# A graph network on one core: one group of edges in five picked by one-hot products, picked rows summed by two additions, lines compared two groups ahead

## What is computed

```
# layer 0, per edge: msg from the source row, weighted by a score of both rows and the relation
a   = tanh(relu(sum((x[src] @ A1.T + b1) * (x[dst] @ A2.T + b2 + rel_emb[etype])) / sqrt(32)))
nei = segment_sum(a * (w_comp[etype] x basis weights applied to x[src]), dst)
x   = layernorm(x + relu(nei + x[src[last edge of the node]] @ self_loop))
x   = layernorm(x + segment_sum(x[src], dst))                    # layer 1
x   = layernorm(x + softmax attention over the edges of a node)  # layer 2
x   = layernorm(x + 10 steps of normalised propagation)          # layer 3
```

## Time and profile before

| | |
|---|---|
| median of 3 runs | 1260.72 us (1260.57 to 1262.55) |
| profiled execution, its own time | 1265.35 us |
| its span, first to last instruction | 1263.6 us |
| mean granted TensorE clock | 0.778 |
| busy: TensorE, VectorE, ScalarE, GpSimd | 977.7, 1020.9, 638.0, 698.4 us |
| first scores of the sweep (L1285) | 63.03 us |
| last gather issued | 912.1 us |
| load of the sums issued (L527) | 929.18 us |

### The profile page before, as it was taken

One profiled execution on the slowest core, in us unless ns is written; L12 is line 12 of the kernel. 1 busy time (PEld: TensorE's weight loads), 2 busy tenths in 40 slices (PEclk: granted clock), 3 DMA queues, 4 the chain that ended last, 5 costly groups with the idle time before them and its releaser, 6 DMA issues.

```text
span 1263.6 us, 58393 instructions
## 1 busy us (share of the span) xinstructions
PE 977.7 (77%) x23808; PEld 898.6 (71%) x23808; DVE 1020.9 (81%) x3443; ACT 638.0 (50%) x1731; POOL 698.4 (55%) x686
## 2 busy tenths in 40 slices
PE   2368788788788787787788677767827995999996
PEld 2357677677677676676677566666726995999996
DVE  8679999889888988898889888888844997655556
ACT  1146666656565555565566555555688980000000
POOL 5777777777777777777777777777600000000000
PEclk9557777777777767767777777767758997999998
DMA  4522222122222221122122212221100000000001
GB/s 108 73 46 56 51 46 46 46 48 48 47 46 46 46 45 45 45 46 45 45 46 46 44 46 45 45 45 41 18 14 3 3 4 3 4 4 4 4 4 18
DMA packets 55896, 46.32 MB, mean 37 GB/s; under 512 B 37442, under 2 KB 51837, under 8 KB 55624
## 3 DMA queue, kind: packets, MB, share of 16 engines
q1 hardware_dynamic: 34056, 31.45, 8.9%
q0 software_dynamic: 21568, 11.09, 6.9%
HBM read 40.19 MB, written 2.28 MB: 34 GB/s over the span
## 4 chain that ended last, share of the span: by engine, by line
PE 25%; DMA 21%; DVE 17%; issue 14%; SPq 11%; POOL 10%; ACT 1%; DVEq 0%; POOLq 0%; ACTq 0%
PE ps L820 12%; POOL arena L587 10%; DMA arena<-line_table 10%; DMA agg_table<-arena 8%; PE ps L762 3%; SPq L519 3%; SPq L496 3%; PE ps L728 3%; DMA arena<-x_pad,arena 3%; DVE arena L1271 2%; SPq L520 2%; SPq L500 2%; DVE arena L1465 2%; DVE arena L1269 1%; PE ps L709 1%
## 5 line engine op out<-in xcount | busy, mean ns | idle before, releaser
L587 POOL DMA_INDIRECT arena<-x_pad,arena x674 | 696.5, 1033 | 205.8 <-issue 200.3
L728 PE MATMUL ps<-arena 128*32 128x44 f32 (+3 forms) x7832 | 204.9, 234 | 152.5 <-DVE arena L1300 152.1
L728 PEld LDWEIGHTS ps<-arena 128*32 128x32 f32 x7832 | 152.4, 133 | 192.7 <-DVE arena L1300 167.3
L1271 DVE TENSOR_SCALAR arena<-pair_no,arena 128x275 bf16<-128x275 f16 (+2 forms) x784 | 239.2, 308 | 0.0
L820 PE MATMUL ps<-arena,adj_words 128*128 128x64 f16 (+1 forms) x6250 | 195.7, 193 | 24.5 <-DVEq L1415 21.8
L820 PEld LDWEIGHTS ps<-arena,adj_words 128*128 128x128 fp8e4 x6250 | 193.5, 98 | 26.6 <-DVEq L1415 22.6
L1300 DVE TENSOR_TENSOR arena<-ps,arena 128x768 f32<-128x768 f32 x196 | 188.0, 959 | 6.7
L709 PE MATMUL ps<-arena 128*128 128x175 bf16 (+3 forms) x1567 | 164.0, 261 | 31.3 <-DVE arena L1271 30.4
L762 PE MATMUL ps<-aggT 128*128 128x128 bf16 x2268 | 175.3, 244 | 0.0
L1015 ACT ACTIVATE arena<-arena 128x4 f32<-128x4 f32 x196 | 40.2, 205 | 266.7 <-DVE arena L1286 255.9
L762 PEld LDWEIGHTS ps<-aggT 128*128 128x128 bf16 x2268 | 159.2, 112 | 0.0
(11 more groups left out here) (213 smaller groups left out, 1261.7 us busy)
## 6 DMA issues: line engine op xcount, KB each, us to landing
arena<-line_table SPq DMA_DIRECT2D x28, 602.0 KB
arena<-x_pad,arena POOLq DMA_INDIRECT x674, 3.3
arena<-line_table SPq DMA_DIRECT2D x28, 140.0 KB
arena<-pick_table SPq DMA_DIRECT2D x27, 128.0 KB
arena<-dst_parts SPq DMA_DIRECT2D x196, 5.7 KB
agg_table<-arena SPq DMA_DIRECT2D x196, 2.5 KB
dst_parts<-aggT SPq DMA_DIRECT2D x1, 735.0 KB, 14.7
x<-x_pad SPq DMA_DIRECT2D x1, 400.0 KB
```

The lines of the kernel that those rows point to most:

```text
L587: pool.indirect_dma_start(to, None, table, bass.IndirectOffsetOnAxis(ap=index, axis=0)).then_inc(done, 16)
L728: return nc.tensor.matmul(to.rearrange("p (d m) -> p d m", m=MIX_COLS)[:, :, 0:m1 - m0], rows_of_slot, factors[:, :, m0:m1], start=False, ...
L1271: last = v.tensor_scalar(pair_hot[:, h, k, 0:n], pair_no[:, 0:n], pair_of[:, g, k:k + 1], None, ALU.is_equal)
```

## The change

One group in five is picked instead of one in seven: groups 7, 12, ..., 192, 38 in place of 27. The order within a pick is as before, but the reading of picked rows now stands ahead of the next one-hots, and both bursts of one-hots move by one group, to the first two groups of each five. The code loads of SyncE leave the branch of the line loads and come every fifth group. The reduction L1324 becomes two additions. Lines are compared two groups ahead instead of four.

```diff
-LINE_AHEAD = 4
+LINE_AHEAD = 2
-PICK_AT, PICKS = LINE + 3, LINES - 1
-PICKED = range(PICK_AT, PICK_AT + PICKS * LINE, LINE)
+PICK_EVERY, PICK_LEAD = 5, 2
+PICK_AT = PICK_EVERY + PICK_LEAD
+PICKED = range(PICK_AT, GROUPS, PICK_EVERY)
+PICKS = len(PICKED)
-HOTS_AT = ((1, range(0, 4)), (2, range(4, PICK_DEEP)))
+HOTS_AT = ((0, range(0, 4)), (1, range(4, PICK_DEEP)))
...
                         if c >= 1:
                             load_lines(c)
-                        if c < PICKS:
-                            if c >= 2:
-                                sp.wait_ge(pick_hots, c - 1)
-                            sp.dma_start(codes[:, c % 2, :], pick_table[c:c + 1, :].to_broadcast([P, WINDOW]))\
-                              .then_inc(code_in[c % 2], 16)
+                    if g % PICK_EVERY == 0 and g // PICK_EVERY < PICKS:
+                        c = g // PICK_EVERY
+                        if c >= 2:
+                            sp.wait_ge(pick_hots, c - 1)
+                        sp.dma_start(codes[:, c % 2, :], pick_table[c:c + 1, :].to_broadcast([P, WINDOW]))\
+                          .then_inc(code_in[c % 2], 16)
...
-                    if g // LINE < PICKS and g % LINE >= LINE - SLOTS:
-                        pick_tile(g // LINE, g % LINE - (LINE - SLOTS))
+                    if g // PICK_EVERY < PICKS and g % PICK_EVERY >= PICK_EVERY - SLOTS:
+                        pick_tile(g // PICK_EVERY, g % PICK_EVERY - (PICK_EVERY - SLOTS))
...
-                    link(v.tensor_reduce(xp[:, PICKED[c] % AHEAD, :, 0:FEAT],
-                                         picked.rearrange("p (k w f) -> p k f w", k=SLOTS, w=PICK_WIDE), AX.X, ALU.add))
+                    of = picked.rearrange("p (k w f) -> p k w f", k=SLOTS, w=PICK_WIDE)
+                    half = PICK_WIDE // 2
+                    link(v.tensor_tensor(of[:, :, 0:half], of[:, :, 0:half], of[:, :, half:PICK_WIDE], ALU.add))
+                    link(v.tensor_tensor(xp[:, PICKED[c] % AHEAD, :, 0:FEAT], of[:, :, 0, :], of[:, :, 1, :], ALU.add))
...
+                    if g % PICK_EVERY == 0 and 1 <= g // PICK_EVERY <= PICKS:
+                        read_picked(g // PICK_EVERY - 1)
                     for group, (at, _) in enumerate(HOTS_AT):
-                        if g % LINE == at and g // LINE < PICKS:
-                            make_pick_hots(g // LINE, group)
-                    if g % LINE == 0 and 1 <= g // LINE <= PICKS:
-                        read_picked(g // LINE - 1)
+                        if g % PICK_EVERY == at and g // PICK_EVERY < PICKS:
+                            make_pick_hots(g // PICK_EVERY, group)
                     make_mixed(g)
```

More of the change, by code:

```diff
@@ L1211, in _ @@
             dve.sem_inc(codes_made, 1)
-            link(v.tensor_scalar(pick_of, block_of[:, PICK_AT::LINE, :][:, 0:PICKS, :], PICK_WIDE - 1, None, ALU.bitwise_and))
+            link(v.tensor_scalar(pick_of, block_of[:, PICK_AT::PICK_EVERY, :], PICK_WIDE - 1, None, ALU.bitwise_and))
             for w in range(PICK_WIDE):
@@ L1822 @@
         "x_pad": x_pad, "edges": edges,
-        "src_cols": columns(grouped[:, 0]), "pick_rows": grouped[:, 0].reshape(GROUPS, WINDOW)[PICK_AT::LINE][:PICKS], "dst_cols": columns(grouped[:, 1]), "next_cols": columns(after), "bases": bases,
+        "src_cols": columns(grouped[:, 0]), "pick_rows": grouped[:, 0].reshape(GROUPS, WINDOW)[PICK_AT::PICK_EVERY], "dst_cols": columns(grouped[:, 1]), "next_cols": columns(after), "bases": bases,
         "dst_rows_in": grouped[:, 1].reshape(LINE_ROWS, -1), "rel_rows_in": grouped[:, 2].reshape(LINE_ROWS, -1),
```

## The result

The changed kernel takes 1252.20 us (median of 6 runs, 1248.47 to 1255.37) beside 1260.99 for the kernel before (6 runs, 1258.91 to 1263.63): a ratio of 0.9926, 95% interval 0.9905 to 0.9948, or 8.8 us less. Its profiled execution took 1252.85 us, with a span of 1250.6 and a mean granted clock of 0.842 (1263.6 and 0.778 before).

What follows compares the result with a forecast made beforehand. SyncE's queue, whose line loads hold its stores, was taken to set the end. Start -4.3, last line-load wait -1.7, tail -4, code loads -1 gave -11: 1260.7 - 11 = 1249.7 us, range 1236 to 1261.5.

Steps and rivals of the forecast that it cites:

- The start: SyncE's early line loads, up to the one at 180.52 us: issued 4.3 us earlier, bounds 1 and 6.
- The lines' lead: Lines compared two groups ahead: VectorE's 7.0 us wait in group 3 goes, so SyncE's early line loads come earlier.
- The added picks: One more set of one-hots and extra reading of picked rows by group 20: 2.7 us off the start's gain.
- The cycles: SyncE's 22 line-load cycles: -1.7 us for the wait before the last line load, -1 for the moved code loads.
- The tail: SyncE's 25 stores after the last line load: 4 us less waiting, bounds 0 and 7.6.
- The gathers' end: GpSimd's gathers end near 874 us: 44 fewer save 55, 11 more one-hot sets cost 16, so 39 gained.
- VectorE's wait for the sums: At the sweep's end VectorE waits for the sums longer than 10.97 us, by 15 us or more.
- The rule on two additions: Two-input additions contend with GpSimd's reads: 0.70 us in each of 38 picks, 27 us more for the gathers.
- The new wait: SyncE's code loads wait for VectorE's one-hots: expected to end before it starts; seeing such waits would show the forecast wrong.
- B: Rival: the gathers' relief is passed on, the end moves with the sweep by -19 to -39 us, 1222 to 1242; chance 0.12.
- C: Rival: nothing is left, code loads cost 0.8 us in the open, tail gains nothing; 1258 to 1263 us; chance 0.16.
- D: Rival: slower, TensorE at 1.2 GHz sets the pace, 4.44 us a group; 1273 us or more; chance 0.08.

Runs made afterwards that it cites:

- e1_lines4: The changed kernel with lines compared four groups ahead again instead of two; 1258.44 us, ratio to before 0.9980.
- e9_picks_alone: The changed kernel with lines four groups ahead and the single reduction, leaving only one group in five picked; 1260.37 us, ratio to before 0.9994.
- e10_one_in_six: The changed kernel with one group in six picked instead of one in five; 1252.88 us, ratio to before 0.9934.
- e2_old_lines2: The kernel before with lines compared two groups ahead as its one edit; 1260.12 us, ratio to before 0.9989.
- e4_old_split: The kernel before with each line load of 86 partitions issued as 80 and 6; 1257.59 us, ratio to before 0.9972.
- e3_split: The changed kernel with each line load of 86 partitions issued as 80 and 6; 1224.84 us, ratio to before 0.9711.

## Why the prediction came out

**The bound was right.** In all twelve kernels the span ends 334 to 336 us after SyncE's load of the sums (929.18 to 1263.6 before, 915.52 to 1250.6 after, 864.33 to 1199.8 in the fastest). In the changed kernel that load follows SyncE's queue: making the queue longer costs its full time, taking its hold away gains 27.4 us, and VectorE's 11.7 us and 24 gathers cost nothing.

**The start** (predicted -4.3 us): measured -4.15 at the sixth line load. Its two parts can be read apart. The lines' lead gives 182.39 - 176.37 = 6.0 to 184.24 - 179.14 = 5.1 (7.0 predicted). The added picks take 182.39 - 180.52 = 1.9 with the additions (2.7 predicted), and 184.24 - 180.52 = 3.7 with the reduction, for which the prediction's prices give 2.0 + 1.71 = 3.7. So with the additions the two parts were priced 1.0 and 0.8 us too high and the errors cancel; the match to 0.2 us is in part luck.

**The cycles** (-1.7 for the wait before the last line load, -1 for the code loads): measured -2.84 over the 22, with no wait at a line load over 0.2 us. One execution of each does not settle so small a difference: `e1_lines4`, with the same code loads, took 668.38 us for these cycles where the changed kernel took 673.67.

**The tail** (-4, with 0 and 7.6 as bounds): measured -6.7 from the last line load on, of which 41.33 - 35.51 = 5.8 in the 25 stores. It lies nearer the upper bound; in `e9_picks_alone`, where only the picks differ from before, it is 923.35 - 856.62 = 66.7 us, so 5.4 of the 6.7 come with the picks.

**The median** was predicted at 1249.7 and is 1252.2, for a reason that the sum does not hold. I took the sum from the profiled execution, 4.6 us above the median of its kernel, and carried that offset over. The profile after came out at 1252.85, below the 1254.3 predicted for it, but only 0.65 above its median. So part of what the change took from the profile of before was not there in the ordinary run. The predicted 11 us lie between the 12.5 of the two profiles and the 8.8 of the medians; that the forecast is only 2.5 us off is partly luck.

**The gathers' end** (874 predicted) was mis-sized: 835.8. The excess over 1.25 us a gather is 59 us in 674 before; from 11.3 to 835.8 there are 629 steps of 1.311, an excess of 38 us, though there are 11 more sets of one-hots. So the stretch is not a fixed 1.5 us a set, about 1 at most. The gathers gained 76.3 us, outside the prediction's bounds of 31 and 55. The traces show where: the gathers that overlap a one-hot (L1312 before, L1315 after) take 43.0 us beyond 945 ns each before, 1.6 us a set as the prediction read it, and 26.4 us after, 0.7 a set. It is 0.7 as well without the additions and the lead (`e9_picks_alone`) and with 32 sets (`e10_one_in_six`), and 1.5 in the old order with the lead (`e2_old_lines2`). So it goes with the new order and places of the bursts; why they stretch the gathers less stays open. It did not matter, since the gathers were not the bound. VectorE's wait for the sums is 20.63 us, 9.7 above the 10.97 of before: longer, as named, but not by the 15 that the prediction asked for.

**The rule on two additions** (the Trainium skill, SBUF — State Buffer, "Who interferes with whom"), by which, in the prediction's estimate, they would hold the gathers by 27 us: with the reduction in their place the last gather starts at 834.6 in place of 835.8, in the version with the split at 834.4 in place of 840.2, and with lines four ahead at 835.4 in place of 840.5. At most 6 of the 27 us can be theirs here.

**The new wait** of code loads for one-hots, one of the prediction's signs of being wrong, is there early (29.6 us in 3), and not later (0.5 us). The prediction said that the fifth line load would ask for more anyway, which holds as far as that load comes 4 us earlier than before. With one in six the wait is 7.1 us and that load comes at 144.36 in place of 145.08, so no more than 0.7 us hangs on it.

**The rivals.** B, the gathers' relief passed on, fell with the hold of 12.9 us; with the hold gone it is what happened. C, nothing left, is what each part alone gives, though not for C's reasons. D, TensorE setting the pace, did not come: VectorE waited 6.0 us for it in the sweep.

What the prediction missed is how near the gathers lay to SyncE's queue. It costed the lines' lead as a gain of its own, 4.3 us with or without the picks. `e2_old_lines2` gives 0.9 of it (at most 3.0 by its interval), because there SyncE waits for the sweep, which the gathers hold. `e4_old_split` agrees: with SyncE's hold gone from the kernel before, no more than 3.4 us are gained.

## What to carry to other kernels

When two chains end within a few microseconds of each other, a change to either alone can show nothing, and a change to both be worth more than the sum; so try the parts together before one of them is called useless. The chain of waits follows one thread, so test the engine that it names by giving it work: here VectorE stood at 40% of it and 11.7 us more work there cost nothing. A queue that issues serially and waits for each of its stores turns one slow transfer into a delay for all behind it, and shortening that transfer was worth 27.4 us in the changed kernel, three times as much as the change itself. In the kernel before it was worth 3.4, because the gathers stood right behind it.

## What the runs showed of the hardware

A transfer to 86 partitions lay between two stores that came 12.9 us apart, and with the same bytes sent as 80 and 6 partitions they came 4.3 us apart (`e3_split`). The Trainium skill (DMA: Bandwidth & Descriptors, "Why a DMA increments its semaphore by 16 and not by 1") has a transfer use the largest number of engines up to 16 that divides its slowest dimension: that would be 2 for 86 and 16 for 80. The traces record every DMA packet, and they agree. The line load issued at 757.74 in the changed kernel and the one of 20 partitions behind it move 106 rows of 7,168 bytes from 758.63 to 772.21, and for 11.3 of these 13.6 us just two rows are under way. In `e3_split` the rows of the load issued at 761.15 take 4.2 us (762.08 to 766.25), with 16 or more under way for 1.7 of them. The 25 loads from 100 us on take 13.0 to 14.9 us each in the one and 3.6 to 5.7 in the other. The records show the hold as well: of the 20 packets of the store issued at 760.73, 16 are through by 761.86 and the last four start at 772.25, right behind the load's last row; SyncE issues the next store at 773.63.

TensorE's granted clock over the sweep rose with the number of picks, from 0.73 with 27 to 0.77 with 32 and 0.82 with 38. The row of the version with one in six, to be read beside the one of the changed kernel above:

```profile
63.00:900.00 837.00, 664.52 (x15302) 596.49 (x15300) 771.51 (x2886) 518.92 (x1611) 611.26 (x616) 0.77 0.20 46
```

TensorE did more pick products (2268, 2688 and 3192), and a larger part of the sweep went at 2.4 GHz. The rival that feared for it at 1.2 GHz assumed that the clock would stay as it was; it rose. The lines' lead has no part in this: with it and 27 picks (`e2_old_lines2`) the clock is 0.73 as before. Why it rose is not shown.

A set of one-hots itself became slower beside the gathers, 360 ns an operation in place of 343, while the gathers were stretched less. What decides which of the two waits, no run here shows.
